# Causal attention on one core: row maxima and scores taken two heads at a time, with one bank for the products instead of two

## The chip, the cores and the metric

The kernel runs on one core of a Trainium2 chip. The metric is device time in microseconds of one execution. The engines named below are PE (TensorE, matrix products), PEld (its weight loads), DVE (VectorE), ACT (ScalarE), POOL (GpSimd) and SP (SyncE, which here only issues transfers). A bank is one of the eight accumulation banks of 128 x 512 fp32 that PE writes and DVE or ACT read.

## The reference, cut to what matters

The input is `x` of shape (2, 2048, 256). It is normalised, and two branches are added to it: an attention with low-rank projections, and a block of attention plus a mixture of 16 experts. Both branches hold the same kind of causal attention, with 16 heads of 16 features over 2048 tokens and 2 batches:

```python
scores = jnp.einsum('bqhd,bkhd->bhqk', Q, K) / math.sqrt(D_K)
scores = jnp.where(causal, scores, -jnp.inf)
attn = jax.nn.softmax(scores, axis=-1)
out = jnp.einsum('bhqk,bkhd->bqhd', attn, V)
```

Two attentions x 2 batches x 4 groups of 4 heads make the 16 groups of which the text speaks.

## The kernel before

The program runs in stages, one after another: constants, stage A (norms, projections, each q and k split into three bf16 parts), stage B (attention), stage C and D (output projection, second norm, router), stage E (experts) and stage F (gather and sum). The change lies in stage B, and in the mask constant that `load_constants` makes for it.

Stage B works through 16 groups of 4 heads. Each head has bf16 stacks: 96 rows for keys (`ks`) and queries (`qs`) hold the products of the parts, and 3 more rows of `qs` hold the negated row maximum in three bf16 parts, against rows of ones in `ks`.

Per group there are two kinds of score products:

- **M**: queries on partitions, used only for the row maxima. `ROW_BLOCKS` lists 160 of them (16 query tiles of 128, 4 heads, up to 4 chunks of 512 keys). PE writes one of 3 `m_banks` (line 535) and DVE takes the maximum over it: line 626 for a full chunk, lines 622 and 623 (a short pause, the mask added and the maximum in one custom instruction, then a read of its accumulator) for the chunk on the diagonal, whose width is 128, 256, 384 or 512.
- **S**: keys on partitions, 160 `SCORE_BLOCKS` in 40 key tiles of 4 heads. PE writes one of 3 `s_banks` (line 521), adds the mask on the diagonal with a product of 128 columns (line 524), and ACT takes the exponential into a ring of 8 `probs` (line 584).

After the 4 S of a key tile, PE multiplies the exponentials by V for the key tile before (**PV**, line 552, four fp32 products in four column groups of the array) into one of 2 `v_banks`. At the end of each of the 4 chunks of 512 queries ACT copies the bank (line 591), PE transposes it (**T**, line 560) and DVE divides by the sums (lines 646 and 649) before SP stores it. When all M of the next group are done, DVE makes `negmax` (line 629), PE transposes it (**N**, line 542), DVE splits it into three parts (lines 635 to 641), and SP writes these with 12 transfers into `qs` (line 464). The first S of the next group waits for these rows.

`group_order` writes out by hand one order for PE, ACT and DVE. Within group g it interleaves the S of g with the M of g+1 (**M**) and, at the end, the first M of g+2 (**E**, `EARLY` of them). Semaphores count what each engine has finished: `m_used` (DVE has read an M bank), `p_ready` (ACT has made an exponential), `p_used` (PE has used four of them), `s_ready`, `m_ready`. A ring of n banks is written as a start value n of the semaphore. Before the first group there is a step with M alone; in the last one there is no M.

Of the kernel before, what the change touches and what calls it, by code (L numbers as in the profile page):

```python
# [15 lines left out]
ALU = mybir.AluOpType  # L16
# [7 lines left out]
P = 128  # L24
# [14 lines left out]
GH = 4  # L39
# [285 lines left out]
EARLY = 16  # L325


def group_order(exps, maxima, carried, early):

    n_m, n_s = len(ROW_BLOCKS), len(SCORE_BLOCKS)
    if not exps and not maxima:
        return [("PV", -1), ("T", -1)]
    if not exps:
        return [("M", m) for m in range(n_m)] + [("N", 0)] + [("E", m) for m in range(EARLY)]
    turn_at = n_s - EARLY - 1  # L340
    last = turn_at - 3
    order, m, e, turn = [], EARLY, 0, None
    for n in range(n_s):
        while maxima and m < n_m and (m - EARLY) * last <= n * (n_m - EARLY):
            order.append(("M", m))
            m += 1
        if maxima and n == turn_at:
            order.append(("N", 0))
        if early and n > turn_at:
            order.append(("E", e))  # L350
            e += 1
        if carried and n in (2, 6):
            order.append(("PV", -1) if n == 2 else ("T", -1))
        order.append(("S", n))
        if n % GH == GH - 1 and n >= GH:
            batch = n // GH - 1
            order.append(("PV", batch))
            if turn is not None:
                order.append(("T", turn))
                turn = None  # L360
            if batch in CHUNK_ENDS:
                turn = CHUNK_ENDS.index(batch)
    return order

ROW_BLOCKS = [(h, t, c) for t in reversed(range(S // P)) for h in range(GH) for c in range(t // TPC + 1)]

SCORE_BLOCKS = [(q, k, h) for q in range(S // CH) for k in range(TPC * (q + 1)) for h in range(GH)]

CHUNK_ENDS = [TPC * (q + 1) * (q + 2) // 2 - 1 for q in range(S // CH)]


def stage_b(nc, scratch, const):

    xin_dram, q_dram, k_dram, v_dram, ctx_dram = scratch
    SLOTS = 3
    NM, NS = len(ROW_BLOCKS) + 1, len(SCORE_BLOCKS)
    NB, NQ = NS // GH, S // CH
    PR = 8
# [4 lines left out]
    with ExitStack() as ctx:  # L390
# [13 lines left out]
        rowmax = sb("rowmax", [P, GH, S // P, NQ])  # L404
        unused = sb("unused", [P, GH, CH], BF16)
# [4 lines left out]
        dve_pause = sb("dve_pause", [P, GH])  # L410
        zeros = sb("zeros", [P, E * CAP * D // P // FILLS])
        m_banks = ctx.enter_context(nc.psum_tensor("m_banks", [P, SLOTS, CH], F32))
# [1044 lines left out]
```

## Time and profile before

| | us |
|---|---|
| Median of 3 runs | 2898.09 |
| Lowest and highest run | 2897.73, 2901.14 |
| Span of the profiled execution | 2894.7 |
| PE busy | 2444.6 |
| DVE busy | 2012.3 |
| ACT busy | 1571.8 |
| Stage B, from its first M to its last T (from 295.1 to 2133.9) | 1838.8 |

The span goes from the first to the last instruction of the profiled execution; the median is of executions measured without the profiler. Busy times are sums over an engine's instructions; a matrix product's time includes the way through the array, so that two that follow each other overlap in the records. The granted clock tells which share of 2.4 GHz PE had.

### The profile page before, as it was taken

The page shows a single profiled execution, that of the slowest core. Times are in us where ns is not written, and L with a number is a line of the kernel's source. Part 1 is how long each engine was busy: PE and PEld are TensorE (multiplying, and loading weights), DVE is VectorE, ACT ScalarE, POOL GpSimd, SP SyncE. Part 2 cuts the span into 40 slices and gives each one's busy share as a digit, 9 for nine tenths or more (in the row PEclk, how much of TensorE's full clock was granted, in tenths as well). Part 3 has the DMA queues.
Part 4 walks back from the last instruction along what each step waited for, and adds up shares of the span by engine and source line. Part 5 has one row for each costly group of instructions (what it writes and reads, how often), then busy time and mean ns, then how long its engine had stood idle before and what let it go on. Part 6 is the DMA issues. An engine that isn't in the chain of part 4 may idle for free. (4 is left out here: it accounts for less than half of the span.)

```text
span 2894.7 us, 52029 instructions
## 1 busy us (share of the span) xinstructions
PE 2444.6 (84%) x15097; PEld 1180.6 (41%) x15097; DVE 2012.3 (70%) x6011; ACT 1571.8 (54%) x3204; POOL 310.4 (11%) x268
## 2 busy tenths in 40 slices
PE   4882899999999999999999999999878407999940
PEld 2541133333333333333333333333237306999930
DVE  4872998888878888888878888888015615666632
ACT  2551047677667777677667677677742103555410
POOL 2445000000000000000000000000013270000034
PEclk9996579999999999999999999999988658999975
DMA  4778640440440440430421321400035104443338
GB/s 126 243 241 189 188 63 3 67 66 4 67 64 6 65 62 9 66 50 21 66 43 29 66 40 31 65 7 5 7 75 138 36 11 153 137 138 130 123 76 113
DMA packets 247944, 223.62 MB, mean 77 GB/s; under 512 B 87124, under 2 KB 224670, under 8 KB 247568
## 3 DMA queue, kind: packets, MB, share of 16 engines
q1 hardware_dynamic: 236944, 193.80, 29.3%
q0 software_dynamic: 10752, 26.80, 4.4%
q8 instruction: 121, 1.98, 0.3%
q14 instruction: 127, 1.04, 0.1%
HBM read 142.63 MB, written 83.89 MB: 78 GB/s over the span
## 5 line engine op out<-in xcount | busy, mean ns | idle before, releaser
L584 ACT ACTIVATE probs<-s_banks 128x512 f32<-128x512 f32 (+3 forms) x2560 | 1210.5, 541 | 503.1 <-PE s_banks L521 252.9
L626 DVE TENSOR_REDUCE rowmax<-m_banks 128x1 f32<-128x512 f32 x1536 | 998.5, 686 | 149.7 <-PE m_banks L535 141.7
L535 PE MATMUL m_banks<-ks,qs 96*128 96x512 bf16 (+3 forms) x2560 | 922.8, 367 | 91.0 <-DMA vs<-v_scratch 59.9
L521 PE MATMUL s_banks<-qs,ks 99*128 99x512 bf16 (+3 forms) x2560 | 865.5, 351 | 15.0 <-ACT probs L584 12.8
L552 PE MATMUL v_banks<-probs,vs 128*32 128x512 f32 (+3 forms) x5120 | 600.3, 541 | 0.0
L535 PEld LDWEIGHTS m_banks<-ks,qs 96*128 96x128 bf16 x2560 | 249.8, 98 | 773.0 <-DVE rowmax L626 362.9
L623 DVE CUSTOM_DVE_ANT_0 unused<-m_banks,c_maskq 128x512 bf16<-128x512 f32 (+3 forms) x1024 | 486.9, 487 | 108.0 <-issue 105.9
L521 PEld LDWEIGHTS s_banks<-qs,ks 99*128 99x128 bf16 x2560 | 248.3, 98 | 177.6 <-ACT probs L584 80.9
L524 PE MATMUL s_banks<-c_maskk,c_identb 128*128 128x128 bf16 x1024 | 223.8, 221 | 0.0
L734 POOL TENSOR_TENSOR c_xn<-c_xn,c_ob 128x1024 f32<-128x1024 f32 x8 | 18.8, 2350 | 1854.3 <-DMA c_xs<-in_L_attn_x 1854.3
L1257 PE MATMUL e_banks<-w_parts,hid_parts 128*128 128x256 f32 x1536 | 188.0, 284 | 0.0
L1257 PEld LDWEIGHTS e_banks<-w_parts,hid_parts 128*128 128x128 f32 x1536 | 185.3, 192 | 0.1
L1242 PE MATMUL e_banks<-xinT,w_parts 128*128 128x512 f32 x768 | 179.6, 393 | 5.1 <-DVE w_parts L1156 5.1
L552 PEld LDWEIGHTS v_banks<-probs,vs 128*32 128x32 f32 x5120 | 100.8, 108 | 169.9 <-ACT probs L584 87.9
L1242 PEld LDWEIGHTS e_banks<-xinT,w_parts 128*128 128x128 f32 x768 | 144.8, 190 | 35.2 <-issue 5.5
L1210 ACT ACTIVATE hid_parts<-e_banks,c_b1T 128x512 fp32r<-128x512 f32 x128 | 89.5, 699 | 110.6 <-PE e_banks L1242 103.7
L524 PEld LDWEIGHTS s_banks<-c_maskk,c_identb 128*128 128x128 bf16 x1024 | 101.8, 99 | 85.2 <-issue 4.1
L1177 DVE TENSOR_TENSOR hid_parts<-e_hid,hid_parts 128x512 fp32r<-128x512 f32 x128 | 87.7, 691 | 58.0 <-ACT e_hid L1211 57.1
L219 POOL TENSOR_TENSOR parts<-rest,parts 128x512 bf16<-128x512 f32 x64 | 92.3, 1442 | 142.2 <-DVE parts L194 142.2
L646 DVE RECIPROCAL inv<-v_banks 128x16 f32<-128x16 f32 x64 | 16.4, 256 | 128.5 <-PE v_banks L560 128.5
L1211 ACT ACTIVATE e_hid<-e_banks,c_b1T 128x512 f32<-128x512 f32 x128 | 88.9, 694 | 0.0
L1229 PE MATMUL e_banks<-c_ident,xin 128*128 128x128 f32 x128 | 17.5, 282 | 81.4 <-DMA xin<-xin_scratch 81.4
(181 smaller groups left out, 1698.2 us busy)
## 6 DMA issues: line engine op xcount, KB each, us to landing
w<-in_L_ffn_fc_w SPq DMA_DIRECT2D x32, 1024.0 KB, 5.3
qs<-q_scratch SPq DMA_DIRECT2D x96, 256.0 KB, 17.4
v_scratch<-vt SPq DMA_DIRECT2D x64, 256.0 KB, 4.0
vs<-v_scratch SPq DMA_DIRECT2D x32, 512.0 KB, 23.0
q_scratch<-parts SPq DMA_DIRECT2D x96, 128.0 KB
k_scratch<-parts SPq DMA_DIRECT2D x96, 128.0 KB
ks<-k_scratch SPq DMA_DIRECT2D x16, 768.0 KB, 7.8
ks<-k_scratch SPq DMA_DIRECT2D x16, 512.0 KB, 10.1
```

Source lines behind the costliest of these rows:

```text
L219: pool.tensor_tensor(parts[:, slot, 2, :], rest[:, slot, :], parts[:, slot, 1, :], ALU.subtract).then_inc(lo_ready, 1)
L521: ins = pe.matmul(bank, ks[:, now, h, k * P:(k + 1) * P], qs[:, now, h, q * CH + first:(q + 1) * CH], start=True, stop=not diagonal)
L524: ins = pe.matmul(bank[:, 0:P], const["identb"][:, :], const["maskk"][:, :], start=False, stop=True)
L535: ins = pe.matmul(bank, qs[0:PAIR_ROWS, nxt, h, t * P:(t + 1) * P], ks[0:PAIR_ROWS, nxt, h, c * CH:c * CH + width], start=True, stop=True)
L552: ins = pe.matmul(v_banks[rows, q % 2, first:CH], vs[:, v % SLOTS, k, rows], probs[:, (n * GH + h) % PR, 0:CH - first], start=k == 0, stop ...
L584: act.activation(probs[:, n % PR, 0:width], s_banks[:, (u * NS + n) % SLOTS, 0:width], ACT.Exp, scale=SCALE).then_inc(p_ready, 1)
L623: dve.tensor_tensor_reduce(unused[:, n % GH, 0:width], scores, const["maskq"][:, CH - width:CH], 1.0, NEG, ALU.add, ALU.max, rowmax[:, h, ...
L626: dve.tensor_reduce(rowmax[:, h, t, c:c + 1], scores, AX.X, ALU.max).then_inc(m_used, 1)
L1210: act.activation(hid_parts[:, HI, f, :], bank, ACT.Gelu, bias=bias)
L1211: act.activation(hid[:, f % HRING, :], bank, ACT.Gelu, bias=bias).then_inc(hid_ready, 1)
L1242: last = pe.matmul(banks[:, HBANK + f % HRING, :], w1_parts[:, a, h, f * P:(f + 1) * P], xinT[:, b, h, :], start=h == 0 and (a, b) == PASS ...
L1257: last = pe.matmul(banks[:, OBANK + n, j * D:(j + 1) * D], hid_parts[:, a, f, tile * P:(tile + 1) * P], w2_parts[:, b, f, :], start=f == 0 ...
```

## The change

`EARLY` goes from 16 single M to 8 pairs. M and S are done for two heads at a time.

- M: `m_banks` becomes a ring of 2 pairs of banks. PE fills both banks of a pair (two heads, same queries and keys), and adds the diagonal mask with a product of 128 columns on each (new line 541). One `tensor_reduce` over both banks (new line 629) takes the place of two instructions on DVE; the custom instruction, its pause and the reading of its accumulator go. `maskq` becomes a bf16 tile of 128 x 128.
- S: the ring keeps 3 banks, but PE and ACT deal with pairs. PE waits once for both banks of a pair and signals once after both; ACT waits once for the pair.
- PV: one `v_bank` in place of two; `probs` has 16 slots in place of 8. After a chunk's end the order holds back PV until the copy (C), the transpose (T) and the division (D) are through.
- N uses the first M bank, after the first two E pairs have been issued on DVE; PE's third E pair waits until DVE has made the parts (`mrows_ready`).
- The transfers that clear `xin_scratch` (POOL) wait until the first PV is done.

```diff
-EARLY = 16
+EARLY = 8
+PAIRS = GH // 2
+MROW_UNITS = [(pr, t, c) for t in reversed(range(S // P)) for pr in range(PAIRS) for c in range(t // TPC + 1)]
...
+    order = []
+    ends = ([-1] if carried else []) + CHUNK_ENDS
+    for n in range(n_t):
+        turn_at = n_t - EARLY // 2
+        units = [("E", 2 * (n - turn_at) + j) for j in range(2)] if n >= turn_at and early else \
+            [("M", EARLY + 2 * n + j) for j in range(2)] if n < turn_at and maxima else []
+        if n - 3 in ends:
+            order.append(("D", ends_name(n - 3)))
+        order.append(("S", 2 * n))
+        if n - 2 in ends:
+            order.append(("C", ends_name(n - 2)))
+        order += units[:1]
+        if n - 4 in ends:
+            order.append(("PV", n - 2))
+        order.append(("S", 2 * n + 1))
+        order += units[1:]
+        if n == turn_at and maxima:
             order.append(("N", 0))
+        if n - 2 in ends:
+            order.append(("T", ends_name(n - 2)))
+        elif n - 3 in ends:
+            order.append(("PV", n - 2))
+        elif n > 0 or carried:
+            order.append(("PV", n - 1))
...
+    MRING, SRING = 2, 3
-    PR = 8
+    PR = 16
...
                     if what == "S":
-                        pe.wait_ge(p_ready, at(i, u, NS, n + 1))
+                        pe.wait_ge(p_ready, at(i, u, NS, 2 * n + 2))
+                        pair = [s_banks[:, (u * NS + 2 * n + half) % SRING, 0:CH - first] for half in range(2)]
-                        ins.then_inc(s_ready, 1)
+                        ins.then_inc(s_ready, 2)
...
                         pe.wait_ge(m_used, at(i, v, NM, n + 1))
+                        if what == "E" and n == MRING:
+                            pe.wait_ge(mrows_ready, at(i, u, 1, 2))
+                        diagonal = c == t // TPC
+                        for half in range(2):
+                            h = 2 * pr + half
+                            ins = pe.matmul(bank[:, half, 0:width], qs[0:PAIR_ROWS, nxt, h, t * P:(t + 1) * P],
+                                            ks[0:PAIR_ROWS, nxt, h, c * CH:c * CH + width], start=True, stop=not diagonal)
+                            if diagonal:
+                                ins = pe.matmul(bank[:, half, width - P:width], const["identb"][:, :], const["maskq"][:, :],
+                                                start=False, stop=True)
                         ins.then_inc(m_ready, 1)
...
+                        dve.tensor_reduce(rowmax[:, v % SLOTS, 2 * pr:2 * pr + 2, t, c:c + 1], m_banks[:, (v * NM + n) % MRING, :, 0:width],
+                                          AX.X, ALU.max).then_inc(m_used, 1)
...
+            pool.wait_ge(p_used, AHEAD + 1)
             fill = xin_dram.rearrange("(f p r) d -> f p (r d)", f=FILLS, p=P)
```

PE's row of instructions for a key tile in the middle of a group, before: M and S alternate singly, and each waits for a bank of its own.

```order
L535 MATMUL m_banks<-ks,qs 128x384 [waits m_used]
L519 REGISTER_ALU
L521 MATMUL s_banks<-qs,ks 128x512 [waits p_ready]
L534 REGISTER_ALU
L535 MATMUL m_banks<-ks,qs 128x512 [waits m_used]
L519 REGISTER_ALU
L521 MATMUL s_banks<-qs,ks 128x512 [waits p_ready]
L534 REGISTER_ALU
L535 MATMUL m_banks<-ks,qs 128x256 [waits m_used]
L519 REGISTER_ALU
L521 MATMUL s_banks<-qs,ks 128x512 [waits p_ready]
```

The same place on PE after the change (line 519 is S, 538 is M, 541 the new mask, 560 is PV):

```order
L519 MATMUL s_banks<-qs,ks 128x512 [waits p_ready]
L519 MATMUL s_banks<-qs,ks 128x512
L532 REGISTER_ALU
L538 MATMUL m_banks<-ks,qs 128x512 [waits m_used]
L538 MATMUL m_banks<-ks,qs 128x512
L514 REGISTER_ALU
L519 MATMUL s_banks<-qs,ks 128x512 [waits p_ready]
L519 MATMUL s_banks<-qs,ks 128x512
L532 REGISTER_ALU
L538 MATMUL m_banks<-ks,qs 128x256 [waits m_used]
L541 MATMUL m_banks<-c_maskq,c_identb 128x128
L538 MATMUL m_banks<-ks,qs 128x256
```

Between the two waits for `p_ready` of a key tile there is now one pair of S and one pair of M, and both S products of a pair stand behind one wait.

DVE's row of instructions around the splitting of the row maxima, before (620s are the diagonal M, 629 makes `negmax`, 635 to 641 split it):

```order
L629 TENSOR_REDUCE negmax<-rowmax 128x64 [waits m_used]
L633 REGISTER_ALU
L634 ISA [waits m_ready]
L635 CAST mrows<-m_banks 64x128 [waits mrows_in]
L636 ISA
L637 TENSOR_TENSOR mrest<-m_banks,mrows 64x128 [waits m_step]
L638 REGISTER_ALU
L639 CAST mrows<-mrest 64x128 [waits m_used]
L640 REGISTER_ALU
L641 TENSOR_TENSOR mrows<-mrest,mrows 64x128 [waits m_step]
L619 REGISTER_ALU
```

And after the change (633 makes `negmax`, 629 is the maximum over a pair, 639 to 645 split):

```order
L633 TENSOR_REDUCE negmax<-rowmax 128x64 [waits m_used]
L628 REGISTER_ALU
L629 TENSOR_REDUCE rowmax<-m_banks 128x2 [waits m_ready] x2
L637 REGISTER_ALU
L638 REGISTER_ALU [waits n_ready]
L639 CAST mrows<-m_banks 64x128 [waits mrows_in]
L640 REGISTER_ALU
L641 TENSOR_TENSOR mrest<-m_banks,mrows 64x128 [waits m_step]
L642 REGISTER_ALU
L643 CAST mrows<-mrest 64x128 [waits m_step]
L644 REGISTER_ALU
L645 TENSOR_TENSOR mrows<-mrest,mrows 64x128 [waits m_step]
```

Two maxima over pairs now stand between `negmax` and its splitting, and on PE the transpose N stands behind the second of these pairs.

## Rows read from the trace of the kernel before

**Rows 1.** Busy time of each engine by stretch, in us (x instructions), then the clock.

```profile
core 0: us, PE busy (x) PEld busy (x) DVE busy (x) ACT busy (x) POOL busy (x), PEclk, DMA share, GB/s
300.00:380.40 80.40, 75.18 (x152) 15.70 (x151) 80.37 (x280) 0.00 (x0) 0.00 (x0) 0.50 0.40 133
815.47:930.28 114.81, 110.36 (x723) 40.84 (x721) 92.31 (x301) 77.95 (x165) 0.00 (x0) 0.97 0.27 44
...
831.00:838.00 7.00, 6.89 (x31) 3.17 (x32) 4.16 (x9) 3.96 (x7) 0.00 (x0) 0.52 0.01 5
...
930.28:1038.93 108.65, 107.24 (x723) 39.87 (x721) 91.69 (x301) 77.42 (x165) 0.00 (x0) 1.00 0.29 45
2038.18:2133.50 95.32, 82.19 (x570) 24.36 (x571) 2.72 (x8) 74.95 (x165) 0.00 (x0) 1.00 0.03 6
```

**Rows 2.** Who waited for whom from 600 to 1800: total, times, longest.

```profile
PEld m_banks L535 <- DVE rowmax L626: 227.6, 448, 1.0
ACT probs L584 <- PE s_banks L521: 174.3, 238, 1.1
ACT probs L584 <- PE s_banks L524: 172.8, 241, 4.5
...
PEld s_banks L521 <- ACT probs L584: 13.1, 56, 0.4
```

**Rows 3.** Timeline of PE in one key tile: start, duration, instruction.

```profile
712.24 0.22 PE L524 MATMUL s_banks<-c_maskk,c_identb 128*128 128x128 bf16 x1
...
712.30 0.38 PE L535 MATMUL m_banks<-ks,qs 96*128 96x512 bf16 x1
...
712.52 0.33 PE L521 MATMUL s_banks<-qs,ks 99*128 99x384 bf16 x1
...
713.57 0.22 PE L524 MATMUL s_banks<-c_maskk,c_identb 128*128 128x128 bf16 x1
...
713.72 1.06 PE L552 MATMUL v_banks<-probs,vs 128*32 128x512 f32 x8
...
714.71 0.39 PE L535 MATMUL m_banks<-ks,qs 96*128 96x512 bf16 x1
```

**Rows 4.** Timeline: S, the exponentials after it, the S waiting for their bank.

```profile
760.59 0.38 PE L521 MATMUL s_banks<-qs,ks 99*128 99x512 bf16 x1
...
761.00 2.06 ACT L584 ACTIVATE probs<-s_banks 128x512 f32<-128x512 f32 x4 [0.94 <-PE s_banks L521]
...
2054.83 1.58 ACT L584 ACTIVATE probs<-s_banks 128x512 f32<-128x512 f32 x3 [0.39 <-PE s_banks L521]
2055.47 0.10 PEld L521 LDWEIGHTS s_banks<-qs,ks 99*128 99x128 bf16 x1 [0.81 <-ACT probs L584]
```

**Rows 5.** Groups of instructions by line and shape: busy, mean ns, idle before.

```profile
L584 ACT ACTIVATE probs<-s_banks 128x512 f32<-128x512 f32 x1792 | 941.2, 608 | 316.3 <-PE s_banks L521 252.9 <-PE s_banks L524 61.6
L584 ACT ACTIVATE probs<-s_banks 128x384 f32<-128x384 f32 x256 | 111.9, 493 | 45.9 <-PE s_banks L524 45.7
L584 ACT ACTIVATE probs<-s_banks 128x256 f32<-128x256 f32 x256 | 92.1, 383 | 65.4 <-PE s_banks L524 60.9
L584 ACT ACTIVATE probs<-s_banks 128x128 f32<-128x128 f32 x256 | 66.8, 277 | 75.6 <-PE s_banks L524 70.8
```

**Rows 6.** Timeline of DVE: three maxima over 512, and one over 256.

```profile
295.78 1.89 DVE L626 TENSOR_REDUCE rowmax<-m_banks 128x1 f32<-128x512 f32 x3 [30.08 <-PE m_banks L535]
...
380.40 0.42 DVE L629 TENSOR_REDUCE negmax<-rowmax 128x64 f32<-128x256 f32 x1
```

**Rows 7.** Timeline: the chunk's copy on ACT and transpose on PE.

```profile
721.15 0.60 ACT L591 ACTIVATE pv_sb<-v_banks 128x512 f32<-128x512 f32 x1
...
722.84 0.60 PE L560 MATMUL v_banks<-c_ident,pv_sb 128*128 128x128 f32 x4
...
723.28 0.33 PE L521 MATMUL s_banks<-qs,ks 99*128 99x384 bf16 x1
```

**Rows 8.** Timeline: the maxima's way into the next group's first S.

```profile
707.29 0.33 PE L542 MATMUL m_banks<-c_ident,negmax 128*128 128x128 f32 x1 [0.20 <-DVE negmax L629]
...
719.57 0.38 PE L521 MATMUL s_banks<-qs,ks 99*128 99x512 bf16 x1
...
2028.25 0.28 DVE L635 CAST mrows<-m_banks 64x128 bf16<-64x128 f32 x1 [0.48 <-PE m_banks L542]
...
2029.52 0.51 SPq L464 DMA_DIRECT2D qs<-mrows  x1
...
2038.18 0.39 PE L521 MATMUL s_banks<-qs,ks 99*128 99x512 bf16 x1 [0.39 <-DMA qs<-mrows]
```

**Rows 9.** Timeline of PE: the gap at the end of a loop pass.

```profile
831.11 0.61 PE L535 MATMUL m_banks<-ks,qs 96*128 96x512 bf16 x1 [3.04 <-issue]
```

More of the change, by code:

```diff
@@ L322, in _ @@
                         last.then_inc(unit_ready, 1)
-EARLY = 16
+EARLY = 8
+PAIRS = GH // 2
+MROW_UNITS = [(pr, t, c) for t in reversed(range(S // P)) for pr in range(PAIRS) for c in range(t // TPC + 1)]
+KEY_TILES = [(q, k) for q in range(S // CH) for k in range(TPC * (q + 1))]
+CHUNK_ENDS = [TPC * (q + 1) * (q + 2) // 2 - 1 for q in range(S // CH)]
 def group_order(exps, maxima, carried, early):
-    n_m, n_s = len(ROW_BLOCKS), len(SCORE_BLOCKS)
+    n_m, n_t = len(MROW_UNITS), len(KEY_TILES)
@@ L336, in group_order @@
     if not exps and not maxima:
-        return [("PV", -1), ("T", -1)]
+        return [("PV", -1), ("C", -1), ("T", -1), ("D", -1)]
     if not exps:
[L339 to L347, printed above, removed]
-            order.append(("N", 0))
[L349 to L362, printed above, removed]
@@ L484, in step @@
                 store(i, u, NQ - 1)
-            with sp.Fori(0, 4) as i:
+            with sp.Fori(0, LOOPED // SLOTS) as i:
                 for u in range(SLOTS):
                     step(i, u, i * SLOTS + (u + 2), True)
-            for s in range(12, G - 1):
+            for s in range(LOOPED, G - 1):
                 step(s // SLOTS, s % SLOTS, s + 2, s + 2 < G)
@@ L578, in step @@
                     if what == "S":
-                        q, k, h = SCORE_BLOCKS[n]
+                        q, k = KEY_TILES[n // PAIRS]
                         width = CH - max(k - TPC * q, 0) * P
-                        if h == 0:
-                            act.wait_ge(p_used, at(i, u, NB, n // GH + 1))
-                        act.wait_ge(s_ready, at(i, u, NS, n + 1))
-                        act.activation(probs[:, n % PR, 0:width], s_banks[:, (u * NS + n) % SLOTS, 0:width],
-                                       ACT.Exp, scale=SCALE).then_inc(p_ready, 1)
-                    elif what == "PV" and (n < 0 or n in CHUNK_ENDS):
-                        n, v = (n, u) if n >= 0 else (NB - 1, u - 1)
-                        q = CHUNK_ENDS.index(n)
+                        if n % PAIRS == 0:
+                            act.wait_ge(p_used, at(i, u, NT, n // PAIRS + 1))
+                        act.wait_ge(s_ready, at(i, u, NS, 2 * n + 2))
+                        for half in range(2):
+                            nth = 2 * n + half
+                            act.activation(probs[:, nth % PR, 0:width], s_banks[:, (u * NS + nth) % SRING, 0:width],
+                                           ACT.Exp, scale=SCALE).then_inc(p_ready, 1)
+                    elif what == "C":
+                        q, v = (n, u) if n >= 0 else (NQ - 1, u - 1)
                         act.wait_ge(turned, at(i, v, NQ, q + 1))
-                        act.wait_ge(p_used, at(i, v, NB, n + 1 + PR // GH))
-                        act.activation(pv_sb[:, q % 2, :], v_banks[:, q % 2, :], ACT.Copy).then_inc(pv_copied, 1)
+                        act.wait_ge(p_used, at(i, v, NT, CHUNK_ENDS[q] + 1 + AHEAD))
+                        act.activation(pv_sb[:, q % 2, :], v_bank[:, :], ACT.Copy).then_inc(pv_copied, 1)
             step(0, 0, True, True, False, True)
@@ L1374, in _ @@
                                    pattern=[[-1, P]], channel_multiplier=1).then_inc(made, 1)
-            diagonal = const["maskq"][:, CH - P:CH]
-            pool.affine_select(out=diagonal, in_=diagonal, compare_op=ALU.is_ge, fill=NEG, base=0,
+            pool.affine_select(out=const["maskq"][:, :], in_=const["maskq"][:, :], compare_op=ALU.is_ge, fill=NEG, base=0,
                                pattern=[[-1, P]], channel_multiplier=1).then_inc(made, 1)
```

108 lines of the change are left out of this document (51 added, 57 removed).

## The prediction

> **What bounds the kernel now.** I read the busy times by stretch first, because the change touches stage B alone. A group takes 108.65 us, of which PE is busy 107.24, DVE 91.69 and ACT 77.42, at full clock [rows 1]. The list of waits then says why PE, though nearly always in a record, isn't at its peak: its weight loads for M wait for DVE, 227.6 us in 1200, and ACT waits for PE for 174.3 + 172.8 us [rows 2]. So PE sets the pace, with DVE near behind. ACT has slack, and that slack is what the rest turns on.
>
> What PE must do comes from the distances between starts in the timeline. An M of 512 columns is followed by the next product 0.22 us later (712.30 to 712.52), a mask takes 0.06 (712.24 to 712.30), an S scales with its columns; the PV of a full key tile takes 1.00 us to the next product, and some 0.10 us pass before it (mask at 713.57, PV at 713.72) [rows 3]. For the sums I take 0.213 us for 512 columns and 0.053 for a mask: 512 and 128 columns at the full 2.4 GHz, which the distances round to. A group has 160 M and 160 S with 69,632 columns each: 29.0 us each; 64 masks on S: 3.4; PV: 28 tiles of 1.00 (in a chunk's diagonal the narrower widths add 0.78, 0.57 and 0.35, four times), 40 x 0.10 before them: 38.8; T 4 x 0.45 [rows 7], N 0.3. Together 102.3 us; 6.3 of the 108.65 are waits.
>
> **The change part by part.**
>
> *DVE.* A maximum over 512 takes 0.686 us alone (1.89 us for three, so 0.60 from start to start), one over 256 elements 0.42 [rows 6]. So 256 elements cost 0.266, and one instruction over 2 x 512 takes some 1.13 us from start to start against 1.20 for two. With 56 full pairs and 8 each of 384, 256 and 128 columns the 80 pairs take 77.7 us. With negmax, the splits and divisions some 82 replace the 91.7 of [rows 1]. If a second bank cost as much as a second instruction it would be 86; both ends lie far under PE's time, so DVE falls out of the bound and its waits (part of the 6.3 us) go.
>
> *Masks of M on PE.* 64 products of 128 columns at 0.053: +3.4 us a group. The floor of PE becomes 105.7 us. Even with no wait left, the change would gain 3 us a group.
>
> *S in pairs over three banks.* This is the term that decides. Pair n needs the bank that the first half of pair n-1 used, and PE's one wait for it stands ahead of both products. So PE can't start a pair before ACT has finished the first exponential of the pair before. The chain from the start of one pair to the start of the next has these links. The second product starts 0.21 after the first; from its start to ACT's start pass 0.41 us (760.59 to 761.00); from the start of that exponential to the start of the S that waits for it 0.64 to 0.65 (2054.83 to 2055.47) [rows 4]. Sum 1.28 us. In it PE has one pair of S (0.43) and one of M (0.43, or less): 0.42 us idle. The way from the second pair to the next tile's first holds M and PV, 0.43 + 0.43 + 1.10, longer than the chain, so it doesn't stall. Before, three banks with single steps gave PE two S ahead, and this wait made up 13.1 us in 1200 [rows 2].
>
> For narrower S the chain shortens with the exponential (608, 493, 383, 277 ns [rows 5]) and the products: with the masks, 1.38 us for 512, 1.17 for 384, 0.95 for 256, 0.74 for 128. M's first pair, masks included, fits into it. A group then is:
>
> - first pair to second: 21 full tiles x 1.28 = 26.9; 3 full tiles after a chunk's end, where a PV lies between, 3 x 0.86 = 2.6; diagonal tiles 4 x (1.38 + 1.17 + 0.95) + 3 x 0.74 + 0.6 = 16.8: together 46.3;
> - the second pairs of S: half of 29.0 + 3.4 = 16.2;
> - the second pairs of M: 16 full (0.427), 24 diagonal ones (mean 0.27, + 0.107 of masks): 15.8;
> - PV 38.8, T and N 2.1.
>
> That is 119.2 us.
>
> *One bank for products.* After a chunk's last PV, T stands where the PV of that tile stood. ACT's copy (0.60 [rows 7]) comes behind the first pair's exponentials: 0.63 + 1.03 + 0.62 = 2.28 after the tile's start, while PE reaches T at 2.1. T waits 0.2, and since the copy also pushes the second pair's exponentials back, the next tile's first pair starts some 0.15 late: 0.37 us x 4 = 1.5. The PV held back are done later, at no cost beyond.
>
> *The row maxima.* From ACT and SP nothing changes: DVE's first cast to SP's first transfer 1.27, from there to the waiting S 8.66 us (2029.52 to 2038.18) [rows 8]. But N now comes at the end of the first E tile, 2.35 us after its start, and on DVE the cast stands behind the second E pair, ready at 2.54 and done at 3.7. SP starts at about 4.9 and the rows are in at 13.6. PE's third E pair waits for the split (0.5 us over the chain), and PE then reaches the next group's first S at 12.2: a wait of 1.4 us. Before, S came 12.3 us after N (719.57 against 707.29 [rows 8]), 2 us after the landing. Together 1.9. If PE is slower in these tiles the wait shrinks to nothing; the bound is 0 to 2.5.
>
> Sum of a group: 119.2 + 1.5 + 1.9 = 122.6, or 14.0 over 108.65. There are 15 such intervals: **+210 us**. The three that end a pass of the loop have a gap of 3.04 us and some 7 us at half clock behind it (831.11 [rows 9]; 0.52 from 831 to 838 [rows 1]), 114.81 in place of 108.65 [rows 1]; I leave both as they are.
>
> *The last group*, without M, took 95.3 us at ACT's pace (75 us busy [rows 1]). Now 21 x 1.28 + 3 x 0.43 + 16.4 in the first pairs (the diagonal tiles less the M) = 44.6, 16.2, 38.8, 1.8, and 3.1 at the copies, since no M covers them: 104.5. **+9 us**.
>
> *The first step* (M alone, half clock [rows 1]) took 84.6 us on DVE (295.78 to 380.40 [rows 6]). DVE now needs 78, but at half clock PE makes a pair in 0.85 + some 0.25 of latency, and while DVE has a narrow pair it waits for the next full one (0.25, 0.5, 0.8 us, six times each): about 89. The later clearing of `xin_scratch` frees transfers as the first loads end: 0 to 3 us back. Net **+1**.
>
> Total +220 on a span of 2894.7; the measured median stands 3.4 us over it and I carry that: 2894.7 + 3.4 + 220 = **3118 us**.
>
> **A rule against it.** The clock falls to 0.52 behind a gap of 3.04 us [rows 1, 9]; the last group, in which PE has a record in only 82.2 of 95.3 us, keeps 1.00 [rows 1]. The Trainium skill, "TensorE: Matmul & The Clock Gate", section "A second HAM failure mode: psum-queue depth-cycling", says that PE pausing between groups of products while it cycles through banks can swing between the two clocks. By that rule the 0.42 us pauses would cost more than themselves; by the trace's last group they don't.
>
> **Rivals.**
>
> 1. *The clock falls at the group starts.* The 1.4 us wait for the rows, among the other pauses, draws a stretch at half clock as the loop's gap does. That costs 114.81 - 108.65 - 3.04 = 3.1 us each, in 12 more groups: +37, 3155 us. For: the wait is new. Against: it is half as long as the gap. The rule named above, taken where the pauses of every key tile count, belongs here too.
> 2. *The chain is covered in part.* M and PV arrive such that the wait for the exponential finds it done, say in half the tiles (ACT ahead after the tiles with two PV, narrow M). Half of 40 x 0.42 x 15 goes: about 3000 us. Against: every link of the chain is measured, and nothing stands between the pairs but one pair of M.
> 3. *PE at its floor: faster.* If the exponential of the first half were through before PE has done S and M (0.86 us), no wait would be left, and PE would run at its floor of 105.7 a group, with the last group and the first step as before: 15 x -3.0 = -45, 2853 us. It decides from a chain of 0.86 us; the rows give 1.28.
> 4. *The mask products or the two-bank maximum cost far more than assumed* (a product of 128 columns 0.22 by its record instead of 0.053): 64 x 0.17 x 15 = +160 at most, half of them hidden in the chain. The distances in [rows 3] speak against it.
>
> **How the numbers follow.** Forecast 0.74, rival 1 0.13, rival 2 0.06, rival 3 0.04, rival 4 0.03. The forecast's own bounds are the row wait (0 to 2.5 us a group, -21 to +16), the chain by 0.05 us a tile (+-30), and the first step. The range of 3065 to 3165 takes these and rival 1; it leaves out rivals 2 to 4. A measurement of this kernel can tell about 0.2%, 6 us, from no change. Slower by more than that: 0.94; within: 0.02; faster: 0.04.
>
> **What would show it.** In the changed profile the S of line 519 should wait for ACT's exponential (line 594) once per key tile for about 0.4 us in the list of waits, over 200 us in all. A group should take 122 to 123 us, from one negmax to the next. DVE should be busy about 82 us of it and no longer be waited for by M. The first S of a group should wait 1 to 2 us for `mrows`, and the clock should stay at 1.00 but for the loop's ends. If groups take under 110 us, the chain is wrong; if the clock is below 0.95 in the groups, rival 1 holds.

## The result and the profile after

The changed kernel takes 3179.06 us in the median of 4 runs (3172.71 to 3181.06), against 2898.36 us of the kernel before (4 runs); the ratio is 1.096, with a 95% interval of 1.0944 to 1.0975. That is 281 us slower. I had forecast 220 us slower, 3118 us, in a range that ended at 3165: the direction and the main term held, the size did not.

The page of the changed kernel, its busy times and its granted clock (40 slices of 79 us; the clock in tenths of full speed):

```profile
span 3179.3 us, 47339 instructions
...
PE 2577.6 (81%) x16121; PEld 1214.1 (38%) x16121; DVE 1945.6 (61%) x2683; ACT 1589.2 (50%) x3204; POOL 310.8 (10%) x268
...
PEclk9885599999999999999999999999988855999975
```

Busy time by stretch, the answer to [rows 1]. The first row is the step with M alone. The next three are groups from one `negmax` to the next, the third of them one that ends a loop pass. The fifth is the stretch behind one group's start, and the last is the last group from its first S:

```profile
core 0: us, PE busy (x) PEld busy (x) DVE busy (x) ACT busy (x) POOL busy (x), PEclk, DMA share, GB/s
...
300.00:388.00 88.00, 70.86 (x214) 19.34 (x214) 77.05 (x76) 0.00 (x0) 0.00 (x0) 0.50 0.24 35
...
516.00:640.14 124.14, 114.14 (x793) 40.84 (x785) 87.51 (x94) 78.14 (x165) 0.00 (x0) 1.00 0.26 40
640.14:767.04 126.90, 117.12 (x793) 42.08 (x785) 87.53 (x93) 78.23 (x165) 0.00 (x0) 0.97 0.24 39
893.52:1021.00 127.48, 116.72 (x793) 41.54 (x785) 87.33 (x93) 78.12 (x165) 0.00 (x0) 0.97 0.25 39
...
783.00:790.00 7.00, 6.91 (x36) 3.45 (x37) 4.33 (x4) 3.85 (x9) 0.00 (x0) 0.54 0.00 0
...
2294.90:2416.00 121.10, 93.67 (x571) 24.86 (x572) 2.73 (x8) 78.93 (x165) 0.00 (x0) 0.87 0.02 5
```

A group took 108.65 us and takes 124.1 where the clock stays at 1.00. It does so in 4 of the 15 intervals (123.8 to 125.8 us); most of the others take some 126.9 us at 0.97. DVE is down from 91.7 to 87.5 us a group. The waits of 600 to 1800 us, the answer to [rows 2], have a new first line:

```profile
PEld s_banks L519 <- ACT probs L594: 479.2, 701, 0.8
DVE rowmax L629 <- PE m_banks L538: 257.0, 305, 5.0
ACT probs L594 <- PE s_banks L522: 233.8, 297, 5.7
ACT probs L594 <- PE s_banks L519: 224.3, 428, 1.1
...
PE s_banks L519 <- ACT probs L594: 60.5, 223, 0.5
...
PE s_banks L519 <- DMA qs<-mrows: 22.9, 10, 3.8
```

PE's weight load for S waits 479.2 us for the exponential where it waited 13.1, and in this stretch PE waits in no line for DVE's maxima. DVE, which PE waited for, now waits for PE. The 479.2 us aren't all lost: the weight load waits 701 times in some 380 key tiles, and many of these waits lie while PE is still at PV. In the timeline below the load of 764.41 had waited 0.84 us, and its product comes 1.00 us after the start of PV, as in [rows 3]. What PE itself loses stands better in the distances between the pairs. The timeline of two key tiles (PE, ACT and DVE, some weight loads left out) shows the step itself:

```profile
761.88 1.08 ACT L594 ACTIVATE probs<-s_banks 128x512 f32<-128x512 f32 x2 [0.90 <-PE s_banks L519]
...
762.54 0.61 PE L519 MATMUL s_banks<-qs,ks 99*128 99x512 bf16 x2 [0.35 <-ACT probs L594]
...
764.41 0.60 PE L519 MATMUL s_banks<-qs,ks 99*128 99x512 bf16 x2
...
765.05 1.09 ACT L594 ACTIVATE probs<-s_banks 128x512 f32<-128x512 f32 x2 [0.79 <-PE s_banks L519]
...
765.71 0.60 PE L519 MATMUL s_banks<-qs,ks 99*128 99x512 bf16 x2 [0.46 <-ACT probs L594]
```

The first pair of S starts at 764.41, ACT starts at 765.05 (0.64), the second pair starts at 765.71 (0.66): 1.30 us, for which I had 1.28.

Where the 284.6 us between the two profiled executions lie:

| stretch | before | after | difference | forecast |
|---|---|---|---|---|
| first maximum to first `negmax` | 84.6 | 92.8 | +8.2 | +1 with the loads |
| the 15 intervals between the `negmax` | 1646.9 | 1893.8 | +246.9 | +210 |
| last `negmax` to last division | 107.0 | 134.3 | +27.3 | +9 |
| the stages behind | 760.4 | 762.7 | +2.3 | 0 |

### The profile page after: what moved, and what is told of

Read it like the earlier page. It is cut to its first block and busy times, and to the rows that moved or that the text cites. A ratio compares the mean times of both kernels' runs of the same rounds, so it can differ in the third digit from the quotient of the medians.

```text
span 3179.3 us, 47339 instructions
## 1 busy us (share of the span) xinstructions
PE 2577.6 (81%) x16121; PEld 1214.1 (38%) x16121; DVE 1945.6 (61%) x2683; ACT 1589.2 (50%) x3204; POOL 310.8 (10%) x268
## 5 line engine op out<-in xcount | busy, mean ns | idle before, releaser
L629 DVE TENSOR_REDUCE rowmax<-m_banks 128x2 f32<-128x1024 f32 (+3 forms) x1280 | 1341.2, 1064 | 614.4 <-PE m_banks L538 438.3
L594 ACT ACTIVATE probs<-s_banks 128x512 f32<-128x512 f32 (+3 forms) x2560 | 1226.9, 532 | 759.8 <-PE s_banks L519 380.4
L519 PE MATMUL s_banks<-qs,ks 99*128 99x512 bf16 (+3 forms) x2560 | 741.9, 360 | 175.6 <-ACT probs L594 131.4
L538 PE MATMUL m_banks<-ks,qs 96*128 96x512 bf16 (+3 forms) x2560 | 757.1, 367 | 82.5 <-DMA vs<-v_scratch 53.1
L560 PE MATMUL v_bank<-probs,vs 128*32 128x512 f32 (+3 forms) x5120 | 606.6, 546 | 0.0
L519 PEld LDWEIGHTS s_banks<-qs,ks 99*128 99x128 bf16 x2560 | 186.6, 98 | 918.6 <-ACT probs L594 839.9
L541 PE MATMUL m_banks<-c_maskq,c_identb 128*128 128x128 bf16 x1024 | 213.0, 227 | 0.0
L560 PEld LDWEIGHTS v_bank<-probs,vs 128*32 128x32 f32 x5120 | 101.5, 108 | 192.6 <-issue 150.8
L541 PEld LDWEIGHTS m_banks<-c_maskq,c_identb 128*128 128x128 bf16 x1024 | 103.9, 101 | 41.8 <-issue 0.8
L650 DVE RECIPROCAL inv<-v_bank 128x16 f32<-128x16 f32 x64 | 16.0, 250 | 127.2 <-PE v_bank L568 127.2
```

Of the source, the lines that this page charges most:

```text
L519: ins = pe.matmul(pair[half], ks[:, now, h, k * P:(k + 1) * P], qs[:, now, h, q * CH + first:(q + 1) * CH], start=True, stop=not diagonal)
L538: ins = pe.matmul(bank[:, half, 0:width], qs[0:PAIR_ROWS, nxt, h, t * P:(t + 1) * P], ks[0:PAIR_ROWS, nxt, h, c * CH:c * CH + width], star ...
L541: ins = pe.matmul(bank[:, half, width - P:width], const["identb"][:, :], const["maskq"][:, :], start=False, stop=True)
L560: ins = pe.matmul(v_bank[rows, first:CH], vs[:, v % SLOTS, k, rows], probs[:, (n * GH + h) % PR, 0:CH - first], start=k == 0, stop=k == TP ...
L594: act.activation(probs[:, nth % PR, 0:width], s_banks[:, (u * NS + nth) % SRING, 0:width], ACT.Exp, scale=SCALE).then_inc(p_ready, 1)
L629: dve.tensor_reduce(rowmax[:, v % SLOTS, 2 * pr:2 * pr + 2, t, c:c + 1], m_banks[:, (v * NM + n) % MRING, :, 0:width], AX.X, ALU.max).then ...
```

## The experiments

The theory: one wait and one signal for a pair of S, over a ring of three banks, bind the second pair of a key tile to the exponential of the first. Against it stood the fall of the clock, the changed order with its single bank, and the price of the masks on PE. All kernels compute the whole reference.

### Taking the pair's wait and signal apart

```diff
-                        pe.wait_ge(p_ready, at(i, u, NS, 2 * n + 2))
                         for half in range(2):
                             h = 2 * pr + half
+                            pe.wait_ge(p_ready, at(i, u, NS, 2 * n + 1 + half))
                             ins = pe.matmul(pair[half], ...
...
-                        ins.then_inc(s_ready, 2)
+                            ins.then_inc(s_ready, 1)
...
-                        act.wait_ge(s_ready, at(i, u, NS, 2 * n + 2))
                         for half in range(2):
                             nth = 2 * n + half
+                            act.wait_ge(s_ready, at(i, u, NS, nth + 1))
```

> The changed kernel with the pair's wait and the pair's signal of S taken apart: PE waits for each bank of s_banks by itself and signals after each product, ACT waits for each. Order and rings stay. Theory (the chain over three banks, 1.28 us from first pair to second, sets the pace): the chain falls to 0.41 + 0.65 - 0.21 = 0.86 us, which PE fills with its own work, so some 13 us go from each group: about 3179 - 205 = 2975 us, and the wait of PE for ACT's exponential almost leaves the list. Rival (the time is lost to the falls of the clock at the group starts and to the order with one bank for products): the waits merely move, 3100 to 3180 us.

Measured: 2963.68 us (2960.43 to 2968.92), ratio to the kernel before 1.0228 (1.0211 to 1.0245). Of the 281 us, 215 are gone, with the order, the rings, the masks and the single bank unchanged. A group takes 111.8 us at full clock, 12.3 less. The 205 us of the expectation were for the groups; of the 215, the 15 intervals hold 192 (185 at full clock, the rest from falls of the clock that are gone) and the last group 23. In the timeline, one tile's four exponentials run in a row again, and the second pair starts 0.79 us after the first (here M's first pair is 256 wide):

```profile
681.28 0.60 PE L519 MATMUL s_banks<-qs,ks 99*128 99x512 bf16 x2
681.71 2.06 ACT L594 ACTIVATE probs<-s_banks 128x512 f32<-128x512 f32 x4 [0.77 <-PE s_banks L519]
...
682.07 0.69 PE L519 MATMUL s_banks<-qs,ks 99*128 99x512 bf16 x2
```

One sign did not come: the weight load's wait for the exponential was to almost leave the list, and it is still there:

```profile
PEld s_banks L519 <- ACT probs L594: 326.6, 542, 1.0
```

So this line alone doesn't measure the chain. PE's own wait for the exponential, 60.5 us in 223 waits in the changed kernel, is down to a single one of 0.7 us.

### Half of it: the signal alone

The same without the two lines on `p_ready`: PE waits for a pair, but signals for each S.

> The changed kernel with the signal alone taken apart: PE still waits once for both banks of a pair, but signals after each S, and ACT waits for each. Theory: the chain from first pair to second is 0.41 + 0.65 = 1.07 us in place of 1.28, so half of what the full split gives: some 7 us a group, about 3065 us. Rival (not the chain): no change, 3179 us.

Measured: 3056.51 us (3053.12 to 3058.66), ratio 1.0543 (1.0525 to 1.0561): 123 us off the changed kernel. The second pair starts 1.08 us after the first:

```profile
707.26 0.61 PE L519 MATMUL s_banks<-qs,ks 99*128 99x512 bf16 x2
707.69 2.16 ACT L594 ACTIVATE probs<-s_banks 128x512 f32<-128x512 f32 x4 [0.80 <-PE s_banks L519]
708.34 0.60 PE L519 MATMUL s_banks<-qs,ks 99*128 99x512 bf16 x2
```

A chain of 1.28, 1.07 and 0.86 us as worked out goes with groups of 124.1, 116.9 to 118.8 and 111.8 us, and with times of 3179, 3057 and 2964 us. The chain is what sets most of the lost time.

### The pair's wait put into the kernel before

```diff
-                        pe.wait_ge(p_ready, at(i, u, NS, n + 1))
+                        if n % 2 == 0:
+                            pe.wait_ge(p_ready, at(i, u, NS, n + 2))
...
-                        ins.then_inc(s_ready, 1)
+                        if n % 2 == 1:
+                            ins.then_inc(s_ready, 2)
...
-                        act.wait_ge(s_ready, at(i, u, NS, n + 1))
+                        if n % 2 == 0:
+                            act.wait_ge(s_ready, at(i, u, NS, n + 2))
```

> The kernel before with one thing of the change alone: PE waits for the banks of two S at once and signals after the second, ACT waits for two. Order, rings and masks as before. Theory (the pair's wait over three banks is the cause): between first and second pair of a tile, with one M inside the pair, the chain is 0.43 + 0.41 + 0.65 = 1.49 us against 0.86 us of work, so a group takes some 128 us in place of 108.65 and the kernel about 3195 us. Rival (pairs alone are harmless, the changed order and the single bank do it): 2900 to 2950 us.

Measured: 3241.63 us (3237.06 to 3244.1), ratio 1.1204 (1.1185 to 1.1223). This part alone, put into the kernel before, costs more than the whole change. The timeline has the forecast chain, 880.85 to 882.35, 1.50 us:

```profile
880.85 0.38 PE L522 MATMUL s_banks<-qs,ks 99*128 99x512 bf16 x1
...
881.29 0.38 PE L522 MATMUL s_banks<-qs,ks 99*128 99x512 bf16 x1
...
881.70 1.08 ACT L587 ACTIVATE probs<-s_banks 128x512 f32<-128x512 f32 x2 [0.78 <-PE s_banks L522]
882.35 0.39 PE L522 MATMUL s_banks<-qs,ks 99*128 99x512 bf16 x1 [0.63 <-ACT probs L587]
```

A group takes this long:

```profile
642.41:771.72 129.31, 111.76 (x722) 38.90 (x721) 94.26 (x302) 78.39 (x164) 0.00 (x0) 1.00 0.23 38
```

The time is 47 us over my expectation. A group takes 129.3 us where I had some 128, which is 20 us in 15, and the last group takes 130.2 us from its `negmax` (107.0 before), 14 more than the 9 that the expected total has for it. Of the remaining 13, some 7 lie in the intervals that take longer than 129.3 us (up to 136.0), which lose more than their like did before, and 5 in that the profiled execution, at 3237.06 us, is the fastest of the four.

### N ahead of the first E pair

```diff
-        if n == turn_at and maxima:
-            order.append(("N", 0))
...
             order.append(("C", ends_name(n - 2)))
+        if n == turn_at and maxima:
+            order.append(("N", 0))
         order += units[:1]
...
-                        if what == "E" and n == MRING:
+                        if what == "E" and n == 1:
                             pe.wait_ge(mrows_ready, at(i, u, 1, 2))
...
-                        pe.transpose(m_banks[:, 0, 0, 0:P], negmax[:, :], const["ident"][:, :]).then_inc(n_ready, 1)
+                        pe.transpose(m_banks[:, 1, 0, 0:P], negmax[:, :], const["ident"][:, :]).then_inc(n_ready, 1)
```

> The changed kernel with the transpose N and the splitting of the row maxima placed ahead of the first E pair (into the second bank pair; the second E pair waits for the parts). Theory: the wait of 1.7 to 2.5 us for the rows at each group's first S goes, and if that wait is what brings the 7 us at half clock, the clock stays at 1.00 in the groups that do not end a loop pass; 4 to 5 us a group, 3095 to 3120 us. Rival (the clock falls because of the pauses of every key tile): the wait goes but the falls stay, 2 us a group, about 3145 us.

Measured: 3134.39 us (3127.7 to 3136.22), ratio 1.0808 (1.079 to 1.0826), 45 us off the changed kernel. The time lies outside the 3095 to 3120 us of the theory and nearer to the 3145 us of the rival; the 15 intervals give back 45 us, 3 each, where 4 to 5 were expected. What decides between the two is the clock in the groups. Three groups in a row, all at full clock:

```profile
512.53:634.29 121.76, 114.19 (x793) 40.72 (x785) 87.53 (x93) 78.13 (x165) 0.00 (x0) 1.00 0.24 40
634.29:755.97 121.68, 114.13 (x793) 40.73 (x785) 87.53 (x93) 78.14 (x165) 0.00 (x0) 1.00 0.24 40
755.97:877.80 121.83, 114.15 (x793) 40.73 (x785) 87.53 (x93) 78.14 (x165) 0.00 (x0) 1.00 0.25 40
```

Behind the first group's start and up to the last `negmax` the half clock is left only at the three ends of a loop pass, as in the kernel before. So in the groups the pause in every key tile alone doesn't bring the fall: those pauses are all still here, and the falls went with the wait for the rows. The wait itself looks so in the changed kernel (with N at its first place):

```profile
779.36 0.64 PE L560 MATMUL v_bank<-probs,vs 128*32 128x256 f32 x8
781.68 0.10 PEld L519 LDWEIGHTS s_banks<-qs,ks 99*128 99x128 bf16 x1 [2.17 <-issue]
781.68 0.39 PE L519 MATMUL s_banks<-qs,ks 99*128 99x512 bf16 x1 [1.69 <-DMA qs<-mrows]
```

The next products follow at half clock (0.54 from 783 to 790, above). The wait doesn't always bring a fall, and its length doesn't tell when. Eleven groups of the changed kernel neither follow the first step nor a loop's end. All of them wait 1.5 to 2.2 us for the rows; behind five of these waits the clock is at half for about 7 us, behind two for about 3.4, behind four not at all, the longest among them:

```profile
1036.14 0.39 PE L519 MATMUL s_banks<-qs,ks 99*128 99x512 bf16 x1 [2.18 <-DMA qs<-mrows]
...
1036.14:1048.00 11.86, 11.41 (x92) 4.98 (x92) 9.66 (x10) 6.54 (x18) 0.00 (x0) 1.00 0.33 59
```

In the kernel with the full split, where the pauses in the key tiles are nearly gone and the wait is still there, the clock falls in two of these eleven groups, behind 1.95 and 2.39 us; eight waits of 1.35 to 1.44 us and one of 2.23 us keep 1.00:

```profile
741.14 0.39 PE L519 MATMUL s_banks<-qs,ks 99*128 99x512 bf16 x1 [1.40 <-DMA qs<-mrows]
```

So taking away the wait ends these falls, and taking away the pauses, which also shortens the wait, ends most of them. Whether the pauses have a part in them isn't shown.

The late rows cost 2.4 us of wait (124.14 to 121.7) and 2.8 us of clock (126.9 to 124.14) in a group with a fall of 7 us.

### Both together

> The split of e1_split_both and the early N of e3_early_n together. Theory: both gains add up, PE is at its floor of some 106 us a group, 2870 to 2900 us, level with the kernel before or just under it. Rival (DVE or the one bank for products binds next): above 2950 us.

Measured: 2931.31 us (2928.07 to 2935.42), ratio 1.0111 (1.0094 to 1.0128). A group at full clock takes 109.8 to 111.0 us, and PE is in a record nearly always, as 110 us from the middle of the kernel show:

```profile
600.00:710.00 110.00, 108.53 (x786) 43.12 (x785) 84.74 (x93) 75.40 (x164) 0.00 (x0) 1.00 0.27 45
```

The 45 us of the early N shrank to 32 on top of the split. The result lies between my two cases and in neither: it is 31 us over the 2900 us of the theory and under the 2950 us of the rival. A group stands some 4 us over the 106 us that I took for PE's floor; which waits these are was not settled. What is left over the kernel before, in the same comparison, is 32 us.

### The masks of M back on DVE

On top of the two edits, the products of line 541 go, and DVE takes a diagonal pair with two custom instructions; a full pair stays one maximum. For room, the clearing of `xin_scratch` uses 32 transfers of half the size; its part in the time was not tested by itself.

```diff
+                        if c == t // TPC:
+                            for half in range(2):
+                                slot = 2 * (n % 2) + half
+                                dve.memset(dve_pause[:, slot:slot + 1], 0.0)
+                                last = dve.tensor_tensor_reduce(unused[:, 2 * (n % 2) + half, 0:width], m_banks[:, (v * NM + n) % MRING, half, 0:width],
+                                                                const["maskq"][:, CH - width:CH], 1.0, NEG, ALU.add, ALU.max,
+                                                                rowmax[:, v % SLOTS, 2 * pr + half, t, c:c + 1])
+                            last.then_inc(m_used, 1)
```

> e4_both_early with the masks of M back on DVE: the 128-column products on M go, and DVE takes the two diagonal banks of a pair with the custom instruction of the kernel before, full banks still by one maximum over the pair (the clearing of xin_scratch uses 32 transfers of half the size, for room). Theory (e4 is at PE's floor, DVE has slack): the 64 products at 0.055 us leave the path, 3.5 us a group, and some 4 us in the first step at half clock: about 2875 us, under the kernel before. Rival (DVE becomes the bound, 86 of 106 us busy and each narrow diagonal pair twice as many instructions): 2930 us or more.

Measured: 2892.21 us (2890.54 to 2904.19) against 2896.09 of the kernel before in the same comparison; ratio 0.9995 (0.9983 to 1.0008). It is 39 us under the kernel with both edits (36 when each is held against the kernel before of its own comparison), and not to be told from the kernel before. The expected 2875 us, under the kernel before, did not come. The shortest groups, at full clock, take 107.4 us, 1.3 less than before:

```profile
604.73:712.12 107.39, 105.95 (x725) 38.08 (x721) 88.21 (x253) 75.78 (x165) 0.00 (x0) 1.00 0.27 46
```

The 15 intervals are 11 us shorter; the first step, 5.2 us later at its `negmax`, and the stages behind, 3.4 us longer, give most of it back.

### The masks on PE, in the kernel before

```diff
                         ins = pe.matmul(bank, qs[0:PAIR_ROWS, nxt, h, t * P:(t + 1) * P],
-                                        ks[0:PAIR_ROWS, nxt, h, c * CH:c * CH + width], start=True, stop=True)
+                                        ks[0:PAIR_ROWS, nxt, h, c * CH:c * CH + width], start=True, stop=c != t // TPC)
+                        if c == t // TPC:
+                            ins = pe.matmul(bank[:, width - P:width], const["identb"][:, :], const["maskq"][:, :],
+                                            start=False, stop=True)
```

DVE then takes a plain maximum over every M bank.

> The kernel before with another part of the change alone: the diagonal masks of M on PE (64 products of 128 columns a group) and a plain maximum over every M bank on DVE, singly. Theory (PE sets the pace, 0.055 us a product): +3.5 us a group, about 2950 us. Rivals: the products cost what their records show (0.22 us), 3000 us and more; or they hide in the 6.3 us of waits for DVE, 2900 to 2910 us.

Measured: 2930.65 us (2928.98 to 2933.16), ratio 1.0129 (1.0112 to 1.0146), 19 us under the expected 2950. A group at full clock takes 111.2 us, 2.6 more than before:

```profile
709.54:820.75 111.21, 110.19 (x787) 43.94 (x785) 90.73 (x173) 77.77 (x165) 0.00 (x0) 1.00 0.28 44
```

So the 3.5 us of products come out as 2.6. The other 0.9 may hide in the waits for DVE, which is still the engine that M waits for:

```profile
PEld m_banks L535 <- DVE rowmax L625: 308.6, 548, 0.9
```

That the products cost 0.22 us, the length of their records, is excluded: by the expectation this would have been 3000 us and more.

### The last group's pauses filled

```diff
-            [("M", EARLY + 2 * n + j) for j in range(2)] if n < turn_at and maxima else []
+            [("M", EARLY + 2 * n + j) for j in range(2)] if n < turn_at and maxima else \
+            [("X", n)] if not maxima else []
...
+                    elif what == "X":
+                        if n == 0:
+                            pe.wait_ge(mrows_ready, at(i, u, 1, 1))
+                        for half in range(2):
+                            pe.matmul(m_banks[:, 0, half, :], qs[0:PAIR_ROWS, now, 2 * half, 0:P], ks[0:PAIR_ROWS, now, 2 * half, 0:CH],
+                                      start=True, stop=True)
```

> The changed kernel, with added work in the last group alone: behind each tile's first S pair PE makes two products of 512 columns into an M bank that nobody reads, where the other groups have their first M pair. Theory (the clock falls in the last group since PE pauses longer there; 0.87 over it, against 0.97 to 1.00 in the groups with M): the added 17 us of products fit into the pauses of 0.85 us, the clock stays nearer to 1.00, and the last group, from its first S to its last division, takes 105 to 112 us in place of 121.7 although it does more; in all 3165 to 3172 us. Rival (the clock falls there whatever PE does, or the group is long for another reason): 121 us or longer, 3179 us or more.

Measured: 3168.64 us (3161.03 to 3170.14), ratio 1.0931 (1.0908 to 1.0954). The last group from its first S, with 80 more products in it:

```profile
2291.17:2406.50 115.33, 103.48 (x652) 31.06 (x652) 3.00 (x10) 78.82 (x165) 0.00 (x0) 0.96 0.02 5
```

It takes 115.3 us in place of 121.7, with more work, and the clock is 0.96 in place of 0.87. The total, 10 us less, lies in the expected 3165 to 3172 us, but in part by luck: the group itself fell by 6.4 us, less than the 10 to 17 I had named, and 3.4 us more lie in the groups ahead, which the edit doesn't touch.

## Why the prediction was right and where it failed

**The bound.** PE set the pace and ACT's slack was what the change spent: right. ACT has the same work a group (78.1 us after, 77.4 before), and PE waits for it.

**The chain.** Right in place and size. 1.28 us was worked out, 1.30 stands in the trace; splitting the pair's wait took 12.3 us off a group where 13 were expected, half the split 7.2 where 7 were, and the part alone in the kernel before costs 346 us. That the full split gave 215 us back where 205 was expected is closer than its parts: 23 of the 215 are the last group's, which the 205 didn't hold. The sign I named was too coarse: the weight loads wait 701 times in 1200 us, not once per key tile, and 542 times still in the split kernel.

A group without the wait for the rows was to take 119.2 + 1.5 = 120.7 us, and takes 121.7: 15 us in 15 groups. The term that was too small is the length of a product: I took 0.213 us for 512 columns though the rows said 0.22, and 0.053 for a mask though they said 0.06. A group has 320 products of M and S and 128 masks, and about half of them lie on PE's path; by this estimate that is near 1 us a group. The distance from first to second pair shows it: 1.30, and 1.41, 1.20, 0.99 and 0.77 in the diagonal tiles, where I had 1.28, and 1.38, 1.17, 0.95 and 0.74.

**DVE.** Forecast at 82 us a group, measured 87.5. A maximum over a full pair takes 1.22 us, as worked out; for the sum I had used the 1.13 from start to start of maxima in a row, and they now come one by one. It was off the path either way. Its waits did go, as forecast.

**Masks.** Forecast 3.4 us a group, at 0.053 each. The experiment in the kernel before has 2.6 us net, near this price, and excludes the 0.22 us of rival 4.

**Row maxima.** The mechanism was right (N behind the second E pair, the rows late for the next first S). I had 1.9 us a group, the runs have 2.4: 7 us in 15 groups.

**The clock: the step that failed.** I wrote that the clock stays at 1.00 but for the loop's ends, by the example of the last group before, and gave the fall at the group starts 0.13 as rival 1. It happened, in part: the wait for the rows is followed by 3.4 or 7 us at half clock in seven of the eleven groups that neither follow the first step nor a loop's end. A fall of 7 us costs 2.8 us (rival 1 had 3.1). Against 15 intervals of the full-clock length, the 15 measured ones lose 1893.8 - 15 x 124.14 = 31.7 us; in the kernel before, 1646.9 - 15 x 108.65 = 17.2 were lost, nearly all of it at the loop's ends. The net is 14 us where rival 1 had 37. The twelve other intervals lose 22 us more than before, since not every group has a fall, and the three at the loop's ends 7 us less (9 in place of 16); that this is because the gap there falls in with the wait for the rows is not shown. The intervals' miss of 37 us is thus 15 (product lengths), 7 (rows) and 15 (clock). The sign that I named for rival 1, a clock below 0.95 in the groups, couldn't show it: 7 us at half clock in 127 us leave 0.97.

**The last group** was the larger miss for its size: 27.3 us in place of 9, of which 1.8 lie before its first S. My 104.5 us from its first S were for a full clock. It had 0.87, and took 121.7:

| last group | PE busy share | granted clock | us, first S to last division |
|---|---|---|---|
| before | 0.86 | 1.00 | 96 |
| split | 0.88 | 0.95 | 99 |
| split, N early | 0.88 | 0.93 | 101 |
| signal split | 0.82 | 0.92 | 108 |
| before, S in pairs | 0.74 | 0.94 | 118 |
| N early | 0.78 | 0.86 | 123 |
| changed | 0.77 | 0.87 | 122 |
| changed, pauses filled | 0.90 | 0.96 | 115 |

Only about half of the miss is the clock. A full key tile in the middle of this group takes 2.89 us at full clock and 4.64 us at half. Where the clock was full, the pairs stand so:

```profile
2309.20 0.61 PE L519 MATMUL s_banks<-qs,ks 99*128 99x512 bf16 x2
2309.90 1.08 ACT L594 ACTIVATE probs<-s_banks 128x512 f32<-128x512 f32 x2 [0.72 <-PE s_banks L519]
...
2310.55 0.60 PE L519 MATMUL s_banks<-qs,ks 99*128 99x512 bf16 x2 [0.75 <-ACT probs L594]
```

From the tiles that ran at full clock I estimate some 112 us for the whole group at full clock. So about 9 of the 17 us over my 104.5 are the clock, and about 8 were missing in my sum: the chain without M is 1.35 us in place of 1.28 (1.5 us in 21 tiles), the chains of the four diagonal tiles of a chunk are 4.6 us in place of 4.1 (2.0 in four chunks), and at the start of a chunk PE stalls once more (1.30 us where its work is 0.88, 1.3 in three chunks). About 3 us are not assigned.

With M in the tile the pauses of 0.42 us left the clock alone; without M they are about 0.9 us (1.35 less the 0.44 of the pair), and the clock falls three times, from 2295, 2336 and 2370. It isn't the wait of 2.1 us for the rows ahead of the group: with the early N that wait is 0.7 us, and the last group has 0.86 and 123.5 us. Filling the pauses brought the clock to 0.96; only the fall at the group's start was left. But these pauses don't always bring a fall. Between the falls, and for 67 us of the kernel before with its S in pairs, the clock is 1.00 with the same pauses:

```profile
2309.00:2335.00 26.00, 18.82 (x140) 5.29 (x132) 0.68 (x2) 18.51 (x42) 0.00 (x0) 1.00 0.02 6
2381.00:2416.00 35.00, 25.87 (x175) 6.31 (x172) 0.00 (x0) 24.63 (x51) 0.00 (x0) 1.00 0.00 1
...
2407.00:2474.00 67.00, 49.29 (x331) 12.22 (x332) 0.68 (x2) 47.88 (x98) 0.00 (x0) 1.00 0.01 3
```

The first two rows are of the changed kernel, the third of the kernel before with S in pairs. The two later falls in the changed kernel both start in the second key tile of a chunk. The row that I argued from was of a group in which PE's pauses were other ones: ACT was full there and PE went from one S to the next. The busy share alone doesn't order the kernels (0.88 has 0.93, 0.86 has 1.00, 0.74 has 0.94), so which feature of the pauses decides is left open. The Trainium skill, "TensorE: Matmul & The Clock Gate", section "A second HAM failure mode: psum-queue depth-cycling", tells of a kernel whose clock swings because PE is briefly idle between groups of products while it cycles through PSUM banks. In this group the trace shows such a swing: 0.87 over the group. In the groups with M it doesn't, where 0.42 us of pause in every key tile left 1.00 in three groups in a row.

**The first step** took 8.2 us more where 4.4 was forecast before the loads, and the loads gave back nothing instead of up to 3 us: the first maximum starts at 295.74, at 295.78 before. DVE's waits for PE were right: they make up 11.2 of the 92.8 us, and the forecast had 89 - 78 = 11. What was too small is DVE's own time, 81.6 us where I had 78. Maxima in a row start 1.16 to 1.20 us apart and not 1.13:

```profile
295.74 8.41 DVE L629 TENSOR_REDUCE rowmax<-m_banks 128x2 f32<-128x1024 f32 x7 [28.85 <-PE m_banks L538]
```

**In sum** 37 (intervals), 18 (last group), 7 (first step) and 2 us (the stages behind) went beyond the 220. Of these some 24 are the clock, 15 in the intervals and about 9 in the last group, and it is the largest part. The range ended at 3165, 47 us over the forecast. That is less than its own parts together, rival 1 (37), the chain's bound (30) and the rows' (16), and it had nothing for the last group, which alone missed by 18.

## What to carry to other kernels

When single steps over a ring are gathered into pairs, count the banks that are left for the step ahead: with three banks, one wait in front of a pair puts the reader's whole latency between the pairs, and that chain can be added up from the old profile and held against the work that stands in it (here 1.28 against 0.86 us). Waiting and signalling per bank leaves the order as it is and gave back 215 of 281 us. A new wait on TensorE is to be priced at its length and, as a rival with a price, for the clock behind it. A stretch that loses its filler work is to be priced apart: here the clock of one stretch did not carry over to another.

## What the runs showed of the hardware that I had not expected

- A wait of 1.7 us between two products (2.17 for the weight load) was followed by 7 us at 0.54 of the clock, and one of 2.18 us in the same kernel was not (1.00 in the 12 us behind it). I had thought of the wait as half of the 3.04 us gap and so harmless. Without this wait, and with the pauses in the key tiles in place, the clock stayed at 1.00 in three groups in a row.
- TensorE did more products in less time once its pauses were filled: 115.3 us with 80 more products of 512 columns, 121.7 without.
- A maximum over two banks in one instruction took 1.22 us for 2 x 512 columns, 0.69 over one bank alone; the second bank cost 0.53 us, no more than 512 elements do by [rows 6] (0.266 for 256). In a row they start 1.16 to 1.20 us apart.
